# Two small GpSimd writes behind every gather of a graph network kernel, in all layers

## The reference

```python
def rgcn_conv(x, edge_index, edge_type, W, root, bias):
    out = x @ root + bias
    for r in range(8):
        mask = edge_type == r
        h = x @ W[r]
        msg = jnp.where(mask[:, None], h[src], 0)
        agg = jax.ops.segment_sum(msg, dst, num_segments=N)
        cnt = jax.ops.segment_sum(mask, dst, num_segments=N)
        out = out + agg / jnp.maximum(cnt, 1.0)[:, None]
    return out

h = jnp.maximum(_layernorm(x), 0)
h = relu(rgcn_conv(h, ..., W1)); h = relu(rgcn_conv(h, ..., W2)); h = relu(rgcn_conv(h, ..., W3))
x = x + h
h = jnp.maximum(_layernorm(x), 0)
g = h + segment_sum(h[src], dst)
g = relu(g @ W1 + b1) @ W2 + b2
return x + batchnorm(g) + h
```

## Time and profile before

| | before |
|---|---|
| median of 3 runs | 1944.0 us |
| the profiled execution, its own time | 1944.79 us |
| its span, first to last instruction | 1942.9 us |
| opening gathers | 22.6 to 90.9 us |
| gathers of layer 0 | 107.6 to 653.6 us |
| gathers of layer 1 | 653.6 to 1285.7 us |
| gathers of layer 2 | 1285.7 to 1889.8 us |
| GpSimd busy | 1197.7 us (62%) |
| TensorE busy | 1121.3 us (58%) |
| VectorE busy | 847.5 us (44%) |
| ScalarE busy | 635.8 us (33%) |

### The profile page before, as it was taken

The page is one execution under the profiler, slowest core; times in us unless marked ns, Lnnn a source line. Parts: engine busy times, 40 slices in busy tenths (PEclk is TensorE's granted clock), DMA queues, the critical chain, the costliest instruction groups (busy, mean ns, idle before and its releaser), DMA issues.

```text
span 1942.9 us, 17586 instructions
## 1 busy us (share of the span) xinstructions
PE 1121.3 (58%) x4604; PEld 819.6 (42%) x4627; DVE 847.5 (44%) x3270; ACT 635.8 (33%) x1147; POOL 1197.7 (62%) x1350
## 2 busy tenths in 40 slices
PE   6778655444444655646464656576445564556577
PEld 2256344333434354534343444446333434344445
DVE  4557465455454235656565665661121212122223
ACT  5400500000000247767776766652001111111133
POOL 5755666666666556666666666645666666666650
PEclk9797765555555655656565655665556675766678
DMA  7642333232332311222222222221111111111111
GB/s 227 200 138 80 89 91 102 84 100 81 101 83 84 96 39 45 76 60 71 60 72 63 71 63 60 72 83 40 48 45 47 46 45 46 45 47 46 47 43 35
DMA packets 80802, 144.19 MB, mean 74 GB/s; under 512 B 24687, under 2 KB 38248, under 8 KB 80696
## 3 DMA queue, kind: packets, MB, share of 16 engines
q0 software_dynamic: 39840, 81.67, 17.1%
q1 hardware_dynamic: 40424, 60.68, 9.1%
q10 hardware_dynamic: 432, 0.64, 0.1%
HBM read 100.23 MB, written 42.67 MB: 74 GB/s over the span
## 4 chain that ended last, share of the span: by engine, by line
another core or an unknown queue 28%; PE 25%; issue 21%; DVE 11%; POOL 8%; ACT 6%; DMA 1%; DVEq 1%; SPq 0%; ACTq 0%; POOLq 0%
POOL rows L1249 8%; PE ps_h L529 6%; PE ps_agg L560 6%; DVE early L1058 5%; DVE sel L962 3%; PE ps_a L647 2%; DVE scratch L1047 2%; PE ps_a L667 2%; ACT scratch L844 2%; PE ps_h L667 2%; PE ps_a L578 2%; PE ps_agg L615 1%; ACT stage L816 1%; PE ps_a L601 1%
## 5 line engine op out<-in xcount | busy, mean ns | idle before, releaser
L1249 POOL DMA_INDIRECT rows<-h_table,idx x1175 | 1115.3, 949 | 627.4 <-issue 341.7
L560 PEld LDWEIGHTS ps_agg<-sel,rows 128*128 128x128 f32 x2764 | 590.2, 281 | 328.2 <-issue 269.6
L560 PE MATMUL ps_agg<-sel,rows 128*128 128x64 f32 (+14 forms) x2764 | 581.5, 345 | 212.9 <-issue 171.9
L962 DVE TENSOR_SCALAR sel<-iota,early,norm 128x64 f32<-128x64 f32 x1178 | 356.5, 334 | 427.3 <-remote 281.1
L647 PE MATMUL ps_a<-scratch 128*128 128x300 bf16 x416 | 164.0, 395 | 268.8 <-DVE early L1058 155.0
L1058 DVE TENSOR_TENSOR early<-ps_a,early 128x300 f32 x416 | 195.7, 470 | 270.1 <-remote 203.2
L844 ACT ACTIVATE scratch<-scratch,ones 128x300 bf16<-128x300 f32 x416 | 221.1, 532 | 177.5 <-remote 148.1
L529 PE MATMUL ps_h<-w_all,xT 128*128 128x512 f32 x300 | 206.9, 798 | 119.5 <-ACT xT L756 65.4
L850 ACT ACTIVATE scratch<-iota,code_lo 128x300 f32<-128x300 f32 x416 | 226.5, 545 | 12.5
L940 DVE TENSOR_SCALAR_CACHE_REDUCE agg_s<-scratch,key_f 128x256 bf16<-128x256 int16 x416 | 193.3, 472 | 42.5 <-issue 32.9
L647 PEld LDWEIGHTS ps_a<-scratch 128*128 128x128 bf16 x416 | 59.6, 143 | 309.2 <-issue 296.8
(11 more groups left out here) (158 smaller groups left out, 740.0 us busy)
## 6 DMA issues: line engine op xcount, KB each, us to landing
h_table<-stage SPq DMA_DIRECT2D x130, 256.0 KB
rows<-h_table,idx POOLq DMA_INDIRECT x1175
scratch<-key_rows SPq DMA_DIRECT2D x26, 544.0 KB
h_table<-scratch SPq DMA_DIRECT2D x20, 256.0 KB
x_rows<-in_x SPq DMA_DIRECT2D x6, 256.0 KB, 6.2
w_all<-in_W SPq DMA_DIRECT2D x3, 512.0 KB, 6.6
x_table<-early SPq DMA_DIRECT2D x6, 256.0 KB, 2.3
out<-early SPq DMA_DIRECT2D x6, 256.0 KB
```

Of the source, the lines that this page charges most:

```text
L560: mm = nc.tensor.matmul(sums_of(L, k)[:, at:at + width], mine, sel[edges, G % SELS, in_window:in_window + width], start=False, stop=(t == ...
L962: done = nc.vector.tensor_scalar(mine, here, dst, weight, ALU.is_equal, ALU.mult)
L1249: pool.indirect_dma_start(rows[:, slot, :], None, table, bass.IndirectOffsetOnAxis(ap=column, axis=0)).then_inc(landed, 16)
```

## The change

The pair of memsets is issued behind every gather, in the opening phase and in all three layers (also where the short tile takes no gather). The pair of tile g writes cells 2(g mod 8) and 2(g mod 8)+1 of a buffer that now has 16 cells. The two writes of a pair don't wait for each other any more: only the second write of every eighth pair raises `s_beat`, and only the first write of the next eight waits for it, which stands behind the gather that follows.

```diff
-        beat = sb("beat", [P, 1])
+        beat = sb("beat", [P, 2 * BATCH])
...
-            beats = itertools.count()
-
-            def pause():
-                made = next(beats)
-                if made:
-                    pool.wait_ge(s_beat, made)
-                nc.gpsimd.memset(beat[:], 0.0).then_inc(s_beat, 1)
+            def pause(g):
+
+                n, at = g // BATCH, 2 * (g % BATCH)
+                if g % BATCH == 0 and n:
+                    pool.wait_ge(s_beat, n)
+                nc.gpsimd.memset(beat[:, at:at + 1], 0.0)
+                done = nc.gpsimd.memset(beat[:, at + 1:at + 2], 0.0)
+                if g % BATCH == BATCH - 1:
+                    done.then_inc(s_beat, 1)
...
                                         ).then_inc(s_fore_row[t // BATCH], 16)
-                pause()
-                pause()
+                pause(t)
...
                         if G in END_TILES:
+                            pause(G)
                             continue
...
                             gather(L, G % SLOTS, idx[:, t:t + 1], s_row[G % SLOTS])
+                        pause(G)
```

More of the change, by code:

```diff
@@ L1 @@
-import itertools
 from contextlib import ExitStack
```

## The result

The changed kernel takes 1957.8 us in the median of 20 runs (1946.7 to 1967.8), the kernel before 1947.5 in 20 runs beside it (1936.5 to 1959.0). The ratio is 1.0072, 95% interval 1.0052 to 1.0093: slower by 0.7%, some 14 us by the ratio and 10.3 us by the two medians, inside the 1% that I called "within". The forecast was 1916, so the sign is wrong, and the range (1880 to 1985) held the time. The profiled execution of the changed kernel has a span of 1955.6 us, against 1942.9.

A forecast was written before the change was run, and what follows sets the result against it. The prediction took GpSimd's gathers to be paced by a hidden service of 1.41 us per gather, plus breaks. Its terms summed as 1944.8 - 24 - 8 + 3 = 1916 us, with an 8-in-10 range of 1880 to 1985.

The forecast's parts named there:

- the distance of 1.32 us: Layers: the pair adds 0.07 us to the 1.25 us between gather starts, cutting the surplus from 0.16 to 0.09.
- Rival A: Layers: no change, the pair vanishes in the idle 0.30 us and breaks come as before; 1944 plus 0 to 3, chance 0.27.
- breaks after 16 or more gathers in layer 1: Sign expected in the profile after: GpSimd's stops in layer 1 come later, where they came after 8 and 12 gathers.
- The worth of a smaller surplus: All layers: GpSimd gets ahead more slowly, breaks less often, and the pace reaches 1.427 us per gather; -24 us, best -44.
- The 1.41: Layers: hidden service time in us behind each gather, taken as fixed, against GpSimd's issue every 1.25 us.
- The line through four cycles: Layer 0: cycles of 8, 12, 20 and 24 gathers take 1.41 us per gather plus 0.43 us per break.
- The layer starts: Starts of the three layers: TensorE's crawl begins 9 gathers later, saving 0 to 12 us in each; -8 us in all.
- The opening phase: Without waits per write its gathers come sooner and TensorE's crawl starts earlier, delaying layer 0; +3 us, range 0 to +21.
- The wait once in eight: GpSimd's wait for s_beat, one gather behind its write, normally costs nothing.
- Rival C: Layers: slower by the wait, breaks at every eighth gather, 1.463 us per gather; +20, with the opening's +3 1967, chance 0.10.
- rival B: Every gather of the layers: writes load the hidden service, 1.48 us per gather; +40, with the opening 1987, chance 0.18.
- The port between VectorE and GpSimd: Rule against the change: writes stand behind VectorE's selections, 0.1 to 0.15 us per pair, making the distance 1.42 to 1.47.

The follow-up runs named there:

- four_writes: The changed kernel with four writes behind every gather in place of two, on 32 cells: 1945.5 us, 0.9986 of the kernel before.
- chained_pairs_3: The kernel before, with its pair of writes (each waiting for the one before) also behind every gather of the layers: 1954.5 us, ratio 1.0049 in the slower condition.
- late_wait_3: The changed kernel with 256 cells, so the wait is for a write 120 gathers back: 1969.3 us, 1.0124 of the kernel before, slower condition.
- layers_only_3: The kernel before with the new pairs in the layers only, its opening phase unchanged: 1932.1 us, ratio 1.0047 in the slower condition.
- after_again: The changed kernel run and traced again in a later session: 1964.3 us, 1.0080 of the kernel before.
- before_again: The kernel before, unchanged, traced a second time in a later session, where it took 1949.4 us.
- open_only_3: The kernel before with the change's pairs in the opening phase only, no write in the layers: 1924.9 us, ratio 1.0004 in the slower condition.
- no_writes: The kernel before without the pairs of its opening phase, so no write anywhere: 1963.8 us, 1.0096 of the kernel before.

## Why the prediction was wrong, point by point

**The step that failed first is the distance of 1.32 us.** I bounded the pair between nothing and 0.11 us per gather and took 0.07, "nearer the opening phase's row: it has the same instructions". It doesn't: those writes wait for each other, and the change takes the waits away. The row without waits was the near one, and by my own arithmetic (0.03 + 0.12 + 0.15, against 0.30) it gave nothing. Measured: 1.25 us in the layers and in the opening. With no more distance there was no smaller surplus, and -24 and -8 us had nothing under them. Rival A had this right. The sign that I had named, breaks after 16 or more gathers in layer 1, didn't come either: they come after 8 and 12, as before.

**The worth of a smaller surplus was wrong as well.** The term is -24 us, and the runs show no gain at all. I took breaks to be the cost and the pace of 1.427 as reachable. four_writes (step 1.298) and chained_pairs_3 (1.366) have the distance that I wanted and a third of the remote waits, and came out at 0.9986 and 1.0049 (the forecast was 0.985), with layer 0 at 1.459 and 1.449 us per gather. The 1.41 isn't a constant of the gather: in the long cycle of the chained pairs it is 1.47. The line through four cycles of one kernel was a good description of that kernel and no law for another. I had named this as what would make the prediction wrong at its root, but expected it to go the other way.

**The layer starts** (-8) fell with the distance. Between the last gather of layer 0 and the first of layer 1 lie 11.4 us before (642.2 to 653.6) and 16.3 after (648.4 to 664.7); in the second pair of traces it is 12.3 before and 8.3 after. So the term has no size that these traces show.

**The opening phase** (+3, range 0 to +21) was sized fairly: 0.0 in the medians (1.0004), between 2.2 us earlier and 6.8 later in two pairs of traces, with an effect of +18 us on the start of layer 0 when every write is taken away.

**The wait once in eight** does stop GpSimd (20.9 us in eleven waits, up to 3.3 us), unlike I said. But late_wait_3, where no such wait can bind, loses no less, and its opening phase stands all the same: GpSimd's writes are held even where they wait for nothing. Rival C is out.

**The loss** has the sign of rival B, but neither its price (+40) nor its mark: layer 0's cycles of 16 still lie on 1.41n + 0.43 within 0.15 us, and I had called B right only on a steeper line. What is shown: in the slower condition the writes of the layers cost 0.5% (layers_only_3), and the wait isn't the reason (late_wait_3). Also shown is that with them the stops come sooner, with the step between gathers the same: the four traces with free pairs in the layers have 0, 0, 1 and 0 cycles of 20 or more gathers in layer 0, the four without any write there 9, 7, 11 and 8. And in layer 0 the further stops account for the further time of its counted stretch:

| traces compared | further breaks in layer 0, at 0.43 us | layer 0, measured | layers 1 and 2, breaks at 0.43 us | layers 1 and 2, measured |
|---|---|---|---|---|
| after, before | 11: 4.7 us | +4.6 | 11: 4.7 us | +0.7 |
| after_again, before_again | 9: 3.9 | +4.2 | 3: 1.3 | +2.7 |
| layers_only_3, open_only_3 | 6: 2.6 | +2.4 | 10: 4.3 | +6.3 |
| four_writes, before_again | 17: 7.3 | +8.2 | 27: 11.6 | +5.1 |
| no_writes, before_again (same layers) | -1: -0.4 | 0.0 | -4: -1.7 | +0.2 |

In layers 1 and 2 the account doesn't come out: no_writes, whose layers are those of before, differs from before_again by -5.3 us in layer 1 and +5.5 in layer 2, so one pair of traces can't show a few us there. The remainder of the loss lies at the starts of the layers and behind the last gather, and changes from pair to pair: it isn't explained. Why writes of 0.12 us inside an idle gap make the stops come sooner is open too: nothing in a trace names the sender of these waits. The Trainium skill, NOTIFIC — the notification-queue block, "Interfaces", says that a full internal FIFO for records pushes back on the producers, and that this can stall an engine. By that rule each added instruction would fill it sooner, with which cycles of 16 instead of 20 go, and the 17 further breaks of four_writes; against it stands chained_pairs_3, with as many writes as the change and 5 breaks less in layer 0 than before. No run here shows such a queue. Every execution whose time is given here also has a recorded span, so no run tells either whether the waits would be there without the recording. The size isn't settled either: the halves give 1.0004 and 1.0047, the whole 1.0072 and 1.0080, late_wait_3 1.0124, in three sessions and the result.

**The port between VectorE and GpSimd** acts, but hardly costs anything here. I compared the start of every write of the changed kernel with what VectorE was doing. 57 of the 2496 writes take more than 0.2 us; 55 of these start inside a `tensor_scalar` of VectorE and 2 inside a cast. Of the 1313 that start while VectorE is idle and the 229 that start inside its addition, not one takes so long. Inside the opening phase's selections (L910, 128x384) the mean is 252 ns in 26 writes, inside those of the layers (L961, 128x64) 134 ns in 445, inside those for the adjacency matrix (L1046) 134 in 153, beside an idle VectorE 118. That agrees with the Trainium skill, SBUF — State Buffer, "Who interferes with whom", which names `cast` and `tensor_scalar` among the operations that can take the pair of ports it shares with GpSimd. The slow pair at 79.45 was thus read rightly, but for its size it was no base for 1197 pairs: over the whole kernel it comes to some 13 us of longer writes (an estimate, 26 x 0.134 + 598 x 0.016), nearly all inside the idle gap. VectorE's selections take 339 ns in the mean against 334 and, in the second trace of before, 338; its additions 471 against 470.

No kernel was faster than before in both conditions. open_only comes nearest: 0.9960 and 0.9967 of before in the faster condition, 1.0004 in the slower one, so the opening's part of the change can be kept and the layers' part left out.

## What to carry to other kernels

A small independent write behind an instruction with an idle gap behind it costs no engine time, and one that waits for the write before it costs its full signal time; take the price from a row with the same waits, not from one with the same instruction. Where all engines stand in "remote" waits together, time the kernel in several sessions before reading it: an effect of under 1% may belong to that condition alone, and have the other sign without it. A wait that grows shorter in the profile isn't a gain until the pace over a whole stage, restart to restart, is shorter too. And a count of events times a price per event that meets the total isn't the account until it meets each stage as well, in more than one pair of traces.

## What the runs showed of the hardware that I had not expected

- The same kernel on the same chip took 1624.4 us in one session and 1924.9 in another, 18% more, with gathers, selections and transfers of equal length. Without the waits the 15 runs of the kernel before in the first session spread by 0.2%, with them the 20 of the result by 1.2%.
- One group of four writes without waits adds 0.05 us to a gather's step (1.298 against 1.249): they start 0.03 us apart, and the next gather follows the end of the last by 0.15 us. Where the second write waits for the first, the pair is 0.27 us long instead of 0.15, and the step 1.365.
- Fewer instructions can take longer: without the opening's 96 writes its last gather began at 81.4 instead of 89.8 us, and layer 0, which waits for the table, began at 123.0 instead of 104.9. TensorE ran 10 matmul records instead of 51 between 40 and 80 us.
- A write of one cell is held up where it starts inside a `tensor_scalar` of VectorE: 252 ns beside one of 384 elements and 134 beside one of 64, against 118 beside nothing.
